# The last norm's energies summed group by group in the gelu stage, the hidden spectra fetched in four column groups, and the joined rows formed inside PSUM

## The chip, the cores and the metric

The kernel runs on one core of a Trainium2 chip. A core has TensorE (PE: matmuls; its weight loads are shown apart as PEld), VectorE (DVE), ScalarE (ACT), GpSimd (POOL) and SyncE (SP, which here only issues DMAs). The engines run their own programs and meet at semaphores. The metric is the device time of one execution in microseconds (us), lower is better.

## The reference, cut to what matters

Everything is float32. Layer 0 takes 4 x 32 images of 128 x 128 pixels and works on low-frequency Fourier spectra (33 columns x 64 rows, complex). The part that the change touches is its end:

```
a  = inorm(p + xa)                                   # p: attention result, xa: input
m  = gelu(inorm(spectral_conv(an, m0cw)) + m0sw * an)        # "hidden" image, an = inorm(a)
m  = inorm(spectral_conv(m, m1cw)) + m1sw * m                # m1: second convolution
x1 = x + inorm(m) * mon_w + mon_b + a                        # layer 0 output
```

An inorm needs the mean and the variance of every image. They are not taken from pixels: by Parseval's theorem the variance of `spectral_conv(m, m1cw)` is the sum over the spectrum of |w|^2 |Y|^2, and its covariance with m is the sum of Re(w) |Y|^2, where Y is the spectrum of the hidden image and w the weights of m1. The sums run over 33 x 64 complex coefficients of each image, with column 0 weighted once, the others twice, and column 0 symmetrised.

## The kernel before

The program is a row of stages, each a block that all engines enter and leave together through a barrier. Within a block, what each engine does is written out in order; nothing else schedules it. Three stages matter.

**Stage 5, the gelu stage** (blocks from L1432 on) walks over the 128 images in 16 groups of 8 (`GI = 8`; group g is quarter u of batch b, g = 4b + u). For each group, in the names of the code:

- POOL `stage` copies the group's spectra from `room` to `ts` (2 buffers, L1457).
- PE `inverse_h` transforms back over rows into PSUM `pz` (L1381), ACT `rows_back` copies to `zs` (L1512), PE `inverse_w` gives pixels in PSUM `pi` (L1389).
- DVE `scale` prepares `pre` from the DMA-loaded `mg` (L1556), DVE `add` adds `pi` (L1562), ACT `gelu` makes the hidden image in `yall` (L1531), and its Square into `sq` (L1534) is summed per image by DVE `sum_squares` (L1567).
- The hidden image is transformed forward: PE `forward_h` into `pf` (L1481), ACT `forward_copy` into `even`, `odd` (L1519, L1520), PE `forward_w` into `pq`, `pw` (L1488, L1489), ACT `sines_copy` (L1526), DVE `copy_out` combines both into the spectrum `yo` (66 x 8 x 64; L1575 to L1577).
- POOL `store` writes `yo` to DRAM `ys` (L1462). SP loads `mg` ahead (L1438) and fetches each batch of four groups back with an image per partition, `yt`, in one DMA per batch (L1443).

The helper `lagged(b, u, k, f)` calls f for group g - k in the turn of group g. So in its turn of group g, ACT does rows_back(g), forward_copy(g-1), gelu(g) with its Square, sines_copy(g-1). DVE does scale(g), sum_squares(g-1), add(g), copy_out(g-1). PE does inverse_h(g), forward_h(g-1), inverse_w(g), forward_w(g-1). POOL does stage(g), store(g-2). An engine takes its list strictly in this order.

**Stage 6, the last norm** (from L1620 on). DVE multiplies `yt` by the weights of m1 in four column groups (`product`, L1107 to L1111, five instructions each) into `zp`. ACT squares and sums `zp` (L1120) and scales the attention spectrum `pa` by its factor g in one pass of 128 x 4224 (L1659). DVE sums zp times yt for the covariance (L1703, L1704). Column 0 goes through PE and back to be symmetrised (L1630, L1632). Two square roots are served by ACT (L180). Then DVE joins `zp * r + pa` in five pieces (`rows_ready`, L1725), PE transposes the 33 columns (L1640), and ACT copies them to `tt`, a view of `room` (L1675). One more matmul spreads a factor (L1644).

**Stage 7** starts with the block after it (SP L1776) and reads `tt`, `yall` and the factors. **Stage 4**, ahead of stage 5, ends like the new stage 6: PE multiplies the columns of `zp` with a diagonal matrix `dg` (L1204), ACT copies the result (L1280).

Of the kernel before, what the change touches and what calls it, by code (L numbers as in the profile page):

```python
# [9 lines left out]
ALU = mybir.AluOpType  # L10
# [34 lines left out]
def constants():  # L45
# [12 lines left out]
    c["ph"] = np.concatenate([np.cos(tp), -np.sin(tp[:, 1:])], 1) / 128  # L58
    c["eh"] = np.concatenate([np.concatenate([np.cos(ph).T, -np.sin(ph).T], 0), np.concatenate([np.sin(ph).T, np.cos(ph).T], 0)], 1)
# [99 lines left out]
class Root:  # L159
# [47 lines left out]
def build(nc, a, c, out):  # L207
# [37 lines left out]
    with top:  # L245
# [1149 lines left out]
        s_yt = sem("hidden_columns_loaded")  # L1395
        s_qh, s_mg7 = sem("p7_matrix_loaded"), sems("p7_images_loaded", 2)
        with ExitStack() as p5:
# [15 lines left out]
            yo = sb("yo5", [2 * KW, GPB, GI, KH])  # L1413
# [10 lines left out]
            s_f1, s_e1, s_f2, s_e2, s_yo = sem("p5_h_transform_done"), sem("p5_h_transform_copied"), sem("p5_w_transform_done"), sem("p5_w_transform_copied"), sems("hidden_spectrum_stored", GPB)  # L1424
# [5 lines left out]
            @block.sync  # L1430
            def _(sp):
                sp.dma_start(ph[:, :], c["ph"]).then_inc(s_ph, 16)  # L1432

                def load(b):
                    for u in range(GPB):
                        g = GPB * b + u
                        wait(sp, s_m5, g + 1 - GPB)
                        sp.dma_start(mg[:, u], mixr[:, bass.ds(g * GI, GI), :]).then_inc(s_mg[u], 16)  # L1438

                def hidden_back(b):  # L1440
                    for q in s_yo:
                        sp.wait_ge(q, 16 * (b + 1))
                    sp.dma_start(yt[32 * b:32 * b + 32].rearrange("p w r h -> p (w r h)"), ys[32 * b:32 * b + 32].rearrange("i m k -> i (m k)")).then_inc(s_yt, 16)  # L1443
                load(1)
                sp.dma_start(room[:, 2 * M2:4 * M2], bass.AP(mpl.tensor, 2 * M2, [[0, 128], [1, 2 * M2]])).then_inc(s_m1, 16)
                load(2)
                hidden_back(0)
                load(3)
                for b in range(1, NB):
                    hidden_back(b)  # L1450

            @block.gpsimd
            def _(pool):
                def stage(b, u):
                    g = GPB * b + u
                    wait(pool, s_s1, g - 1)
                    nc.gpsimd.tensor_copy(ts[:, u % 2], tt[:, :, bass.ds(g * GI, GI)]).then_inc(s_ts, 1)  # L1457

                def store(b, u):
                    g = GPB * b + u  # L1460
                    pool.wait_ge(s_e2, g + 1)
                    pool.dma_start(ys[bass.ds(g * GI, GI)].rearrange("i m k -> m i k"), yo[:, u]).then_inc(s_yo[u], 16)  # L1462
# [6 lines left out]
                store(NB - 1, GPB - 2)  # L1469
                store(NB - 1, GPB - 1)  # L1470
                for q in s_yo:
                    pool.wait_ge(q, 16 * NGRP // GPB)

            @block.tensor
            def _(pe):
# [27 lines left out]
                pe.wait_ge(s_sn, NGRP)  # L1503
                nc.tensor.matmul(pq[:, 0:1], ysq[:, :], ones[:, 0:1], start=True, stop=True).then_inc(s_q5, 1)

            @block.scalar
            def _(act):
# [27 lines left out]

                def body(b):
                    for u in range(GPB):
# [6 lines left out]
                sines_copy(NB - 1, GPB - 1)  # L1544

            @block.vector
            def _(dve):
# [41 lines left out]
                ch = Chain(dve, s_v5)  # L1589
                ch.link(V.tensor_scalar(v1("ysq"), pq[:, 0:1], 1.0 / (HH * WW), None, ALU.mult))  # L1590
# [3 lines left out]
        with ExitStack() as p6:  # L1594
# [8 lines left out]
            tx = sb("t6x", [128, 2, 9, 2, KH])  # L1603
            ta = sb("t6a", [128, 2, 9 * 2 * KH])
            cs = sb("cs6", [128, 128])
            en = sb("en6", [128, 8])
            cr = sb("cr6", [128, 8])
            dg = sb("dg6", [128, NI])
            ps = [pb(f"ptr6_{i}", [128, 512]) for i in range(4)]
            psy = pb("psy6", [128, 512])  # L1610
            pbc = pb("pbc6", [128, 512])
            s_z, s_en = sem("p6_products_ready"), sem("p6_energy_sums_done")
            s_sa, s_cs, s_sc = sem("p6_column0_transposed"), sem("p6_column0_copied"), sem("p6_column0_symmetrised")
            s_pg, s_zp = sem("attention_spectrum_scaled"), sem("p6_spectrum_ready")
# [13 lines left out]
            def _(pe):  # L1628
                pe.wait_ge(s_z, 1)
                nc.tensor.transpose(psy[:, 0:128], zp[:, 0].rearrange("p r h -> p (r h)"), ident[:, :]).then_inc(s_sa, 1)  # L1630
                pe.wait_ge(s_cs, 1)
                nc.tensor.matmul(psy[:, 128:256], cs[:, :], sym[:, :], start=True, stop=True).then_inc(s_sc, 1)  # L1632
                n = 0
                for q, chunks in enumerate(ROWS):
                    pe.wait_ge(s_zp, q + 1)
                    for j in chunks:
                        lo, hi = kw_of(j)
                        wait(pe, s_trc, n - 3)
                        for kw in range(lo, hi):
                            m = nc.tensor.transpose(ps[n % 4][:, 128 * (kw - lo):128 * (kw - lo) + 128], zp[:, kw].rearrange("p r h -> p (r h)"), ident[:, :])  # L1640
                        m.then_inc(s_tr, 1)
                        n += 1
                pe.wait_ge(s_dg, 1)
                nc.tensor.matmul(pbc[:, 0:128], ones[:, :], dg[:, :], start=True, stop=True).then_inc(s_bc, 1)  # L1644

            @block.scalar
            def _(act):
                A = nc.scalar

                def squares(n, src, col, scale=1.0):  # L1650
                    size = math.prod(src.shape[1:])
                    square_sum(act, s_en, n, ta[:, n % 2, 0:size], src, en[:, col:col + 1], scale)

                def product_energy(g, n):
                    lo, hi = max(COLS[g][0], 1), COLS[g][1]
                    act.wait_ge(s_z, g + 1)
                    squares(n, zp[:, lo:hi].rearrange("p w r h -> p (w r h)"), g, ROOT2)
                A.activation(v1("warm6"), ident[:, 0:1], ACT.Sqrt)
                A.activation(pa[:, :, :, :], pa[:, :, :, :], ACT.Copy, scale=v1("g")).then_inc(s_pg, 1)  # L1659
                product_energy(0, 1)  # L1660
                act.wait_ge(s_sa, 1)
                A.activation(cs[:, :], psy[:, 0:128], ACT.Copy).then_inc(s_cs, 1)
                act.wait_ge(s_sc, 1)
                squares(2, psy[:, 128:256], 4)
                squares(3, psy[:, 128:256].rearrange("p (r h) -> p r h", r=2)[:, :, 32], 5)
                for g in range(1, len(COLS)):
                    product_energy(g, g + 3)
                root.serve(act, A, v1("r"))
                root.serve(act, A, v1("t"))
                n = 0  # L1670
                for chunks in ROWS:
                    for j in chunks:
                        lo, hi = kw_of(j)
                        act.wait_ge(s_tr, n + 1)
                        A.activation(tt[:, lo:hi], ps[n % 4][:, 0:128 * (hi - lo)].rearrange("p (j i) -> p j i", i=NI), ACT.Copy).then_inc(s_trc, 1)  # L1675
                        n += 1
                act.wait_ge(s_trc, NC6)

            @block.vector
            def _(dve):  # L1680
                ch = Chain(dve, s_v6)
                V = nc.vector
                r, t, var = v1("r"), v1("t"), v1("var")
                w1, yb_, rest, mean = scalar["m1sw"], v1("ybar"), v1("rest"), v1("offset")
                dve.wait_ge(s_m1, 16)
                for g, (lo, hi) in enumerate(COLS):
                    if g == 0:
# [545 lines left out]
```

## Time and profile before

| | us |
|---|---|
| median of 3 runs | 1052.03 (1050.84 to 1057.9) |
| the profiled execution, device time | 1055.65 |
| its span in the trace | 1054.0 |
| stage 5, first POOL instruction to the last SP issue | 417.52 to 541.45 |
| stage 6, first instruction (ACT) to the first of stage 7 | 542.96 to 580.07 |

| engine | PE | PEld | DVE | ACT | POOL |
|---|---|---|---|---|---|
| busy us of the span | 804.5 | 593.1 | 678.4 | 403.8 | 320.8 |

In a timeline row, the first number is the start in us from the span's start, the second the duration or extent, then engine, source line, operation, what it writes <- what it reads, the shapes, and how many instructions the row merges. In brackets stands how long the engine had been idle before and what ended the wait. A float32 matmul appears as two records. A transpose appears as one.

### The profile page before, as it was taken

The numbers are of one execution on the slowest core, as the hardware profiler recorded it, in microseconds if no ns is written. First come the engines' busy times: TensorE is split into PE (matmuls) and PEld (weight loads), VectorE is DVE, ScalarE is ACT, GpSimd is POOL, SyncE is SP. The second block draws the span as 40 slices with busy tenths as digits, with TensorE's granted clock in tenths as the row PEclk, the third lists the DMA queues.
The fourth block names the chain that finished last, engine by engine and source line by source line (L and its number), as shares of the span: only waits on it lengthen the run. The fifth ranks groups of instructions, "written<-read, shape, count | busy, mean of one in ns | idle before, by whom it ended". The sixth has DMA issues, their size and how long they took to land. (4 is left out here: it accounts for less than half of the span.)

```text
span 1054.0 us, 36890 instructions
## 1 busy us (share of the span) xinstructions
PE 804.5 (76%) x16113; PEld 593.1 (56%) x16113; DVE 678.4 (64%) x1459; ACT 403.8 (38%) x915; POOL 320.8 (30%) x198
## 2 busy tenths in 40 slices
PE   0499296899999955999932899566778777777797
PEld 0366142322222215888822899566777776776786
DVE  4898388778888785466648999745555555553122
ACT  0298252122222344466543566433333333331121
POOL 0023373789999900111100000232222222210000
PEclk9999598799999976899965999878998899898899
DMA  9566643376555430255330676489999999998687
GB/s 365 118 194 159 132 82 105 116 271 190 174 182 176 140 81 5 66 181 122 84 79 0 171 190 179 99 189 252 278 285 286 283 289 284 282 281 178 190 243 210
DMA packets 284673, 189.44 MB, mean 180 GB/s; under 512 B 29396, under 2 KB 275893, under 8 KB 283381
## 3 DMA queue, kind: packets, MB, share of 16 engines
q1 hardware_dynamic: 207411, 139.95, 49.3%
q10 hardware_dynamic: 75138, 44.14, 16.6%
q0 software_dynamic: 2048, 4.36, 2.0%
q8 instruction: 45, 0.74, 0.3%
q14 instruction: 31, 0.25, 0.1%
HBM read 154.50 MB, written 33.07 MB: 178 GB/s over the span
## 5 line engine op out<-in xcount | busy, mean ns | idle before, releaser
L2036 PE MATMUL po<-pa,room 128*32 128x16 f32 x8320 | 147.7, 219 | 66.4 <-DMA room<-_L_conv_weight_imag_dram 36.6
L2036 PEld LDWEIGHTS po<-pa,room 128*32 128x32 f32 x8320 | 144.9, 163 | 74.5 <-issue 63.3
L981 POOL TENSOR_TENSOR q<-lead 128x1536 f32<-128x1536 f32 (+1 forms) x51 | 170.3, 3367 | 29.4 <-POOLq L650 13.8
L1080 DVE TENSOR_TENSOR q<-pw,lead 128x1536 f32<-128x1536 f32 (+1 forms) x85 | 140.9, 1704 | 16.9 <-PE acc L1026 11.9
L1989 POOL COPY cols<-y 128x512 f32<-128x512 f32 x32 | 36.7, 1147 | 324.8 <-PE px L2023 184.8
L1026 PE MATMUL acc<-q,pt 128*32 128x384 f32 (+1 forms) x1088 | 104.2, 495 | 13.1 <-DVE q L1080 13.1
L2177 DVE TENSOR_TENSOR osl<-po,neg 128x128 f32<-128x128 f32 x64 | 18.4, 288 | 133.1 <-ACT neg L2110 133.1
L2110 ACT ACTIVATE neg<-po 128x272 f32<-128x272 f32 x32 | 12.7, 398 | 179.8 <-issue 166.6
L2023 PE MATMUL px<-wbat,cols 128*32 128x130 f32 x2176 | 78.0, 297 | 3.0 <-DVE wbat L2148 3.0
L1026 PEld LDWEIGHTS acc<-q,pt 128*32 128x32 f32 x1088 | 28.1, 110 | 87.5 <-issue 58.3
L2023 PEld LDWEIGHTS px<-wbat,cols 128*32 128x32 f32 x2176 | 68.4, 121 | 3.7 <-DVE wbat L2148 3.1
L1381 PE MATMUL pz<-eh,ts 128*33 128x128 f32 x1024 | 65.6, 282 | 6.0 <-DMA ph<-const_ph_dram 3.7
L920 ACT ACTIVATE ms<-pm,vec 128x512 f32<-128x512 f32 x32 | 22.0, 689 | 123.5 <-PE pm L913 116.1
L1389 PE MATMUL pi<-cw,zs 97*128 97x128 f32 x512 | 65.8, 283 | 2.4 <-ACT zs L1512 1.1
L1381 PEld LDWEIGHTS pz<-eh,ts 128*33 128x33 f32 x1024 | 57.1, 141 | 14.4 <-issue 8.3
L1389 PEld LDWEIGHTS pi<-cw,zs 97*128 97x128 f32 x512 | 61.3, 196 | 4.9 <-ACT zs L1512 3.0
L2202 DVE TENSOR_TENSOR yall<-yall,po 128x1024 f32 (+1 forms) x16 | 19.5, 1222 | 57.9 <-PE po L2064 57.9
L2159 DVE COPY pa<-px 32x260 f32<-32x260 f32 x128 | 49.6, 425 | 5.0 <-PE px L2023 3.6
L885 DVE TENSOR_TENSOR room<-gt,tp 128x1408 f32<-128x1408 f32 x26 | 41.3, 1619 | 8.0 <-PE psc L832 4.4
L2099 ACT ACTIVATE pa<-px 32x260 f32<-32x260 f32 x128 | 41.2, 369 | 9.0 <-PE px L2023 8.3
L392 POOL DMA_DIRECT2D xs<-xst x16 | 14.6, 910 | 93.3 <-ACT xst L426 93.3
L1462 POOL DMA_DIRECT2D ys<-yo x16 | 13.2, 824 | 97.6 <-DVE yo L1577 97.6
(334 smaller groups left out, 1540.3 us busy)
## 6 DMA issues: line engine op xcount, KB each, us to landing
room<-_L_conv_weight_real_dram ACTq DMA_DIRECT2D x32, 520.0 KB, 8.4
room<-_L_conv_weight_imag_dram ACTq DMA_DIRECT2D x32, 520.0 KB, 11.2
room<-_L_conv_weight_real_dram SPq DMA_DIRECT2D x32, 520.0 KB, 6.3
room<-_L_conv_weight_imag_dram SPq DMA_DIRECT2D x32, 520.0 KB, 9.6
lead<-xns SPq DMA_DIRECT2D x64, 192.0 KB, 3.0
lead<-wv SPq DMA_DIRECT2D x16, 576.0 KB, 5.9
yall<-in_x_dram SPq DMA_DIRECT2D x4, 2048.0 KB, 14.6
xd<-in_x_dram SPq DMA_DIRECT2D x16, 512.0 KB, 4.2
```

Of the source, the lines that this page charges most:

```text
L885: V.tensor_tensor(z[:, j % 2, :, 0:NDV], bc(bc(w, 1, NB), 3, NT), bc(xx, 2, NDV), ALU.mult).then_inc(s_z, 1)
L920: nc.scalar.activation(ms[:, u], pm[u][:, :], ACT.Identity, bias=v1("cbeta")).then_inc(s_mc, 1)
L981: nc.gpsimd.tensor_tensor(q2[:, t % 2, :, :, 0:m], bc(weights(blk, n), 2, NB), spectra(blk), ALU.mult).then_inc(s_qp, 1)
L1026: e = nc.tensor.matmul(acc[u][rows, 0:3 * m].rearrange("p (r m) -> p r m", r=3), pt[:, k, rows], qk[:, :, b, 0:m], start=(k == 0), stop=(k ...
L1080: V.tensor_tensor(q1[:, t % 2, :, :, 0:m], bc(pw[t % 4][:, 0:3 * m].rearrange("p (r m) -> p r m", r=3), 2, NB), spectra(blk), ALU.mult).th ...
L1381: m = nc.tensor.matmul(pz[64 * v:64 * v + KW, 128 * i:128 * i + 128], ts[:, u % 2, :, i], eh[:, 128 * v:128 * v + 128], start=True, stop=True)
L1389: m = nc.tensor.matmul(pi[:, 128 * i:128 * i + 128], zs[0:KP, u % 2, i, :], cw[:, :], start=True, stop=True)
L1989: nc.gpsimd.tensor_copy(cols[:, u, 0:2], near if c_ < NCHK - 1 else y1v[:, 0:64:63])
L2023: m = nc.tensor.matmul(px[u][g:g + 32, o:o + 2 * KWF], cols[:, u, q if p == 0 else 3 - q, s, 32 * b:32 * b + 32], wbat[:, b, at:at + 2 * K ...
L2036: e = nc.tensor.matmul(po[u][32 * g:32 * g + 32, 512 * q + 16 * m:512 * q + 16 * m + 16], wsl[u][:, :, q * KWF + KWF - 1 - kw], xsl[u][:, ...
L2099: act.activation(re[:, b].rearrange("i q c w -> i q (c w)"), src[:, b].rearrange("i q c w -> i q (c w)"), ACT.Copy)
L2159: V.tensor_copy(re[:, b].rearrange("i q c w -> i q (c w)"), src[:, b].rearrange("i q c w -> i q (c w)"))
```

## The change

Stage 5:

- The weights of m1 are loaded once more in the layout of `yo` (`tab`), and DVE turns them into two tables `wgt` in 12 small steps (`energy_weights`, in the turn of group 1): |w|^2 and Re(w), with column 0 symmetrised.
- For each group, ACT squares `yo` into `yq` (`square`, lag 2), POOL multiplies `yq` with both tables into `ye` and, in place, `yq` (`weigh`, lag 2), DVE sums each over the rows into `part` (`sum_energies`, two reduces, lag 3). `yo` and `yq` have two buffers, `ye` one. At the end PE sums `part` over its 66 partitions with the weights `mw` in two matmuls: variance and covariance are there when stage 5 ends.
- The store of `yo` moves from POOL to SP. SP issues load(t+4) and store(t-2) in turn t, and the fetch of `yt` as four DMAs per batch, one per column group.

Stage 6 loses all energy sums, the column-0 round trip, the scaling of `pa` and the joins on DVE. For each of the 33 columns PE now adds `pa * diag(g)` and `zp * diag(r)` in PSUM (two matmuls), plus one small matmul for the mean. The columns are taken in the order `TURN`, with six PSUM banks. The first square root needs nothing of `yt`.

```diff
             @block.gpsimd
             def _(pool):
...
-                def store(b, u):
-                    g = GPB * b + u
-                    pool.wait_ge(s_e2, g + 1)
-                    pool.dma_start(ys[bass.ds(g * GI, GI)].rearrange("i m k -> m i k"), yo[:, u]).then_inc(s_yo[u], 16)
+                def weigh(b, u):
+                    g = GPB * b + u
+                    pool.wait_ge(s_yq, g + 1)
+                    if g == 0:
+                        pool.wait_ge(s_wt5, 1)
+                    wait(pool, s_ws, g)
+                    v = yq[:, u % 2]
+                    nc.gpsimd.tensor_tensor(ye[:, :, :], v, bc(wgt[:, 0], 1, GI), ALU.mult)
+                    nc.gpsimd.tensor_tensor(v, v, bc(wgt[:, 1], 1, GI), ALU.mult).then_inc(s_we, 1)
 
                 def body(b):
                     for u in range(GPB):
                         lagged(b, u, 0, stage)
-                        lagged(b, u, 2, store)
+                        lagged(b, u, 2, weigh)
...
             @block.scalar
+                def square(b, u):
+                    g = GPB * b + u
+                    act.wait_ge(s_e2, g + 1)
+                    wait(act, s_ws, g - 1)
+                    act.activation(yq[:, u % 2], yo[:, u % 2], ACT.Square).then_inc(s_yq, 1)
...
                         lagged(b, u, 1, sines_copy)
+                        lagged(b, u, 2, square)
...
             @block.vector
+                def sum_energies(b, u):
+                    g = GPB * b + u
+                    dve.wait_ge(s_we, g + 1)
+                    V.reduce_sum(part[:, 0, bass.ds(g * GI, GI)], ye[:, :, :], axis=AX.X)
+                    V.reduce_sum(part[:, 1, bass.ds(g * GI, GI)], yq[:, u % 2], axis=AX.X).then_inc(s_ws, 1)
...
                         lagged(b, u, 1, copy_out)
+                        if b == 0 and u == 1:
+                            energy_weights()
+                        lagged(b, u, 3, sum_energies)
                 each_batch(body)
                 sum_squares(NB - 1, GPB - 1)
                 copy_out(NB - 1, GPB - 1)
+                for n in (3, 2, 1):
+                    sum_energies(NB - 1, GPB - n)
...
             @block.tensor
-                            m = nc.tensor.transpose(ps[n % 4][:, 128 * (kw - lo):128 * (kw - lo) + 128], zp[:, kw].rearrange("p r h -> p (r h)"), ident[:, :])
+                def rows(n):
+                    pe.wait_ge(s_z, PART_OF[TURN[n]] + 1)
+                    wait(pe, s_trc, n - NBANK + 1)
+                    for kw, o in slots(n):
+                        nc.tensor.matmul(o, pa[:, kw].rearrange("p r h -> p (r h)"), dg[:, 0, :], start=True, stop=False)
+                        m = nc.tensor.matmul(o, zp[:, kw].rearrange("p r h -> p (r h)"), dg[:, 1, :], start=False, stop=(kw > 0))
...
```

The order of instructions shows three places. POOL, stage 5, after the first two copies of `ts`; `ys` and `ye` are the stored spectra and the weighted squares. Before:

```order
L1457 COPY ts<-room 128x264 [waits p5_rows_done]
L1462 DMA ys<-yo 66x8x64 [waits p5_w_transform_copied]
L1457 COPY ts<-room 128x264 [waits p5_rows_done]
L1462 DMA ys<-yo 66x8x64 [waits p5_w_transform_copied]
L1457 COPY ts<-room 128x264 [waits p5_rows_done]
```

The same place of the change:

```order
L1483 COPY ts<-room 128x264 [waits p5_rows_done]
L1492 TENSOR_TENSOR ye<-yq,wgt 66x512 [waits hidden_energies_summed,hidden_spectrum_squared]
L1493 TENSOR_TENSOR yq<-yq,wgt 66x512
L1483 COPY ts<-room 128x264 [waits p5_rows_done]
L1492 TENSOR_TENSOR ye<-yq,wgt 66x512 [waits hidden_energies_summed,hidden_spectrum_squared]
```

Between two copies of `ts`, the issue of a store has given way to two products, and they wait for ACT's square and for DVE's sums.

ACT, stage 5, from the third gelu on in the change (before, the row L1573 is not there, and the others stand in the same order):

```order
L1564 ACTIVATE yall<-pre 128x1024 [waits p5_preactivation_ready]
L1567 ACTIVATE sq<-yall 128x1024 [waits hidden_squares_summed,hidden_ready]
L1559 ACTIVATE sines<-pq 66x256 [waits p5_w_transform_sines_done]
L1573 ACTIVATE yq<-yo 66x512 [waits p5_w_transform_copied]
L1545 ACTIVATE zs<-pz 97x1024 [waits p5_pixels_done,p5_rows_done]
L1552 ACTIVATE even<-pf 128x264 [waits p5_w_transform_done,p5_h_transform_done]
```

The square of `yo` stands behind the gelu, its Square and the sines of the same turn, and ahead of the next `rows_back`.

DVE, stage 5, one turn of the change, from `add` to the next `add` (before, the two reduces of `ye` and `yq` are not there):

```order
L1604 TENSOR_TENSOR pre<-pre,pi 128x1024 [waits p5_mixed_scaled,p5_pixels_done]
L1619 COPY yo<-pw 66x8 [waits hidden_spectrum_squared,p5_sine_part_copied,hidden_spectrum_stored_0,p5_w_transform_done]
L1620 TENSOR_TENSOR yo<-pw,sines 66x8x31
L1621 TENSOR_TENSOR yo<-pw,sines 66x8x32
L1646 TENSOR_REDUCE part<-ye 66x8 [waits hidden_energies_weighted]
L1647 TENSOR_REDUCE part<-yq 66x8
L1598 TENSOR_TENSOR pre<-mg,c1b 128x1024 [waits hidden_ready,p5_mixed_loaded_0]
L1609 TENSOR_REDUCE ysq<-sq 128x8 [waits hidden_squared]
L1604 TENSOR_TENSOR pre<-pre,pi 128x1024 [waits p5_mixed_scaled,p5_pixels_done]
```

The sums stand behind `copy_out` and ahead of the next `scale`.

## Rows read from the trace of the kernel before

**Rows 1.** Waits, 445 to 535 us: engine line <- releaser: us, times, longest us.
```profile
POOL ys L1462 <- DVE yo L1577: 77.9, 14, 6.0
```
**Rows 2.** Timeline, one period of stage 5, part of its rows.
```profile
446.81 0.41 POOL L1457 COPY ts<-room 128x264 f32<-128x264 f32 x1
447.87 1.20 DVE L1562 TENSOR_TENSOR pre<-pre,pi 128x1024 f32<-128x1024 f32 x1
448.59 1.97 PE L1381 MATMUL pz<-eh,ts 128*33 128x128 f32 x32
449.10 1.06 ACT L1531 ACTIVATE yall<-pre 128x1024 f32<-128x1024 f32 x1 [2.66 <-DVE pre L1562]
450.19 1.06 ACT L1534 ACTIVATE sq<-yall 128x1024 f32<-128x1024 f32 x1
...
451.16 0.36 ACT L1526 ACTIVATE sines<-pq 66x256 f32<-66x256 f32 x1
451.42 1.01 ACT L1512 ACTIVATE zs<-pz 97x1024 f32<-97x1024 f32 x1
451.62 0.17 DVE L1575 COPY yo<-pw 66x8 f32<-66x8 f32 x1 [2.55 <-ACT sines L1526]
...
452.36 1.21 DVE L1556 TENSOR_TENSOR pre<-mg,c1b 128x1024 f32<-128x1024 f32 x1
452.48 2.05 PE L1389 MATMUL pi<-cw,zs 97*128 97x128 f32 x16
...
453.49 1.21 DVE L1567 TENSOR_REDUCE ysq<-sq 128x8 f32<-128x1024 f32 x1
...
454.62 1.21 DVE L1562 TENSOR_TENSOR pre<-pre,pi 128x1024 f32<-128x1024 f32 x1
```
**Rows 3.** Timeline, stage 5: POOL's copy for group 3, ACT's gelu of group 2.
```profile
440.10 0.41 POOL L1457 COPY ts<-room 128x264 f32<-128x264 f32 x1
...
442.35 1.06 ACT L1531 ACTIVATE yall<-pre 128x1024 f32<-128x1024 f32 x1 [2.63 <-DVE pre L1562]
```
**Rows 4.** Groups by line and shape, POOL: count | busy us, mean ns | idle before.
```profile
L981 POOL TENSOR_TENSOR q<-lead 128x1536 f32<-128x1536 f32 x48 | 164.9, 3464 | 27.7 <-POOLq L650 13.8 <-PE acc L1026 10.5 <-DMA lead<-wv 3.4
...
L763 POOL TENSOR_TENSOR room<-gt,xrm 128x640 f32<-128x640 f32 x26 | 33.0, 1270 | 12.8 <-PE psc L832 12.8
```
**Rows 5.** Timeline, start of stage 5, PE.
```profile
426.84 3.64 PE L1381 MATMUL pz<-eh,ts 128*33 128x128 f32 x32
```
**Rows 6.** Windows: us, busy (count) of PE, PEld, DVE, ACT, POOL; PEclk; DMA share, GB/s.
```profile
404.50:410.00 5.50, 5.32 (x25) 5.32 (x26) 4.91 (x11) 1.19 (x2) 0.00 (x0) 0.50 0.00 0
410.00:415.00 5.00, 5.00 (x46) 5.00 (x46) 0.00 (x0) 3.15 (x6) 0.00 (x0) 0.99 0.00 0
...
537.00:545.00 8.00, 0.00 (x0) 0.00 (x0) 0.61 (x3) 2.03 (x3) 0.81 (x1) 0.50 0.44 96
```
**Rows 7.** Timeline, end of stage 5 and stage 6, part of its rows.
```profile
537.13 0.41 DVE L1577 TENSOR_TENSOR yo<-pw,sines 66x256 f32<-66x256 f32 x1
...
541.15 0.30 SPq L1443 DMA_DIRECT2D yt<-ys  x1
...
542.96 1.28 ACT L1658 ACT_TABLE_LOAD   x1 [6.73 <-PEq L1397]
...
546.06 0.69 DVE L1107 TENSOR_TENSOR t<-room,yt 128x512 f32<-128x512 f32 x1 [8.45 <-DMA yt<-ys]
...
550.23 0.16 DVE L1694 TENSOR_TENSOR vec<-vec 128x1 f32<-128x1 f32 x1
...
552.74 0.69 DVE L1107 TENSOR_TENSOR t<-room,yt 128x512 f32<-128x512 f32 x1
...
556.53 1.06 ACT L1120 ACTIVATE t6a<-zp 128x1024 f32<-128x1024 f32 x1 [3.94 <-DVE zp L1111]
...
573.99 0.60 ACT L1675 ACTIVATE room<-ptr 128x512 f32<-128x512 f32 x1 [3.11 <-PE ptr L1640]
...
580.07 0.36 SPq L1776 DMA_DIRECT2D pa<-mixd  x1
```

More of the change, by code:

```diff
@@ L1432, in _, with load @@
                 sp.dma_start(ph[:, :], c["ph"]).then_inc(s_ph, 16)
-                def load(b):
-                    for u in range(GPB):
-                        g = GPB * b + u
-                        wait(sp, s_m5, g + 1 - GPB)
-                        sp.dma_start(mg[:, u], mixr[:, bass.ds(g * GI, GI), :]).then_inc(s_mg[u], 16)
+                def load(g):
+                    wait(sp, s_m5, g + 1 - GPB)
+                    sp.dma_start(mg[:, g % GPB], mixr[:, bass.ds(g * GI, GI), :]).then_inc(s_mg[g % GPB], 16)
@@ L1445, in _ @@
[L1445 to L1450, printed above, removed]
+                        sp.wait_ge(q, 16 * (GPB // 2) * (b + 1))
+                    for (lo, hi), q in zip(COLS, s_yt):
+                        sp.dma_start(yt[32 * b:32 * b + 32, lo:hi].rearrange("p w r h -> p (w r h)"),
+                                     ys[32 * b:32 * b + 32, 2 * lo:2 * hi].rearrange("i m k -> i (m k)")).then_inc(q, 16)
@@ new lines, in _ @@
+                for r in range(2):
+                    sp.dma_start(tab[:, r], bass.AP(mpl.tensor, 2 * M2 + r * M2, [[KH, KW], [0, 2], [1, KH]])).then_inc(s_tb, 16)
+                sp.dma_start(mw[:, :], c["mw"]).then_inc(s_tb, 16)
+                for t in range(NGRP + 2):
+                    if t + GPB < NGRP:
+                        load(t + GPB)
+                    if t == 1:
+                        sp.dma_start(room[:, 2 * M2:4 * M2], bass.AP(mpl.tensor, 2 * M2, [[0, 128], [1, 2 * M2]])).then_inc(s_m1, 16)
+                    if t >= 2:
+                        store(t - 2)
+                        if (t - 1) % GPB == 0:
+                            hidden_back((t - 1) // GPB - 1)
@@ L1466, in body @@
                         lagged(b, u, 0, stage)
-                        lagged(b, u, 2, store)
+                        lagged(b, u, 2, weigh)
                 each_batch(body)
[L1469 to L1472, printed above, removed]
+                weigh(NB - 1, GPB - 2)
+                weigh(NB - 1, GPB - 1)
             @block.tensor
@@ L1503, in _ @@
                 pe.wait_ge(s_sn, NGRP)
+                pe.wait_ge(s_ws, NGRP)
+                pe.wait_ge(s_tb, 48)
+                for i in range(2):
+                    nc.tensor.matmul(pq[:, i + 1:i + 2], part[:, i, :], mw[:, :], start=True, stop=True)
                 nc.tensor.matmul(pq[:, 0:1], ysq[:, :], ones[:, 0:1], start=True, stop=True).then_inc(s_q5, 1)
@@ L1648, in _ @@
                 A = nc.scalar
[L1650 to L1657, printed above, removed]
-                A.activation(v1("warm6"), ident[:, 0:1], ACT.Sqrt)
[L1659 to L1667, printed above, removed]
+                A.activation(v1("warm6"), ident[:, 0:1], ACT.Sqrt)
                 root.serve(act, A, v1("r"))
                 root.serve(act, A, v1("t"))
[L1670 to L1677, printed above, removed]
+                for n, j in enumerate(TURN):
+                    lo, hi = kw_of(j)
+                    act.wait_ge(s_tr, n + 1)
+                    A.activation(tt[:, lo:hi], ps[n % NBANK][:, 0:128 * (hi - lo)].rearrange("p (j i) -> p j i", i=NI), ACT.Copy).then_inc(s_trc, 1)
+                act.wait_ge(s_trc, len(TURN))
             @block.vector
```

174 lines of the change are left out of this document (97 added, 77 removed).

## The prediction

> **What bounds the kernel now.** The kernel is a row of stages with barriers between them, so the time is the sum of the stages, and a stage is worth what its own longest wait is worth. I read the engines' shares first, then the waits of stage 5, then its timeline over one period, and last the timeline of stage 6.
>
> Stage 5 repeats every 6.75 us: DVE's `add` starts at 447.87 and again at 454.62 [rows 2]. Two things share that period. One is a loop over ACT and DVE: add to gelu 1.23, gelu to sines 2.06, sines to `copy_out` 0.46, `copy_out` to `scale` 0.74, `scale` to `sum_squares` 1.13, and 1.13 more to the next add. That is 6.75, without slack. The other is PE, which starts `inverse_w` at 452.48, on the heels of the matmuls ahead of it. The reader should look above all at who runs beside whom. PE starts `inverse_h` of group G+1 at 448.59, *before* ACT starts the gelu of group G at 449.10, because POOL had copied the spectra of G+1 at 446.81. POOL looks as if it had room: it waited 77.9 us in this stretch for `yo` [rows 1].
>
> Stage 6 takes 37.1 us from 542.96 to 580.07, of which DVE waits until 546.06 for `yt` (idle 8.45 in all). The rest is nearly all DVE [rows 7].
>
> **The change part by part.** The sum is made against the profiled execution (span 1054.0, device time 1055.65). The median of the runs is 3.6 lower, and I carry the difference over to it.
>
> *The loop that closes.* POOL's list is now stage(G+1) behind weigh(G-2). weigh(G-2) waits for ACT's square(G-2), which stands in ACT's list behind gelu(G), its Square and the sines, and it waits for DVE's sum_energies(G-3), which stands behind add(G) and copy_out(G-1). Both need pixels of group G, which need inverse_h(G), which needs stage(G). So stage(G+1) cannot start before nearly all of group G has passed through every engine. The store that stood there before needed only copy_out(G-2), one turn earlier. Queued behind the waiting POOL instruction is the copy of `ts`, and PE waits for that. Nothing else runs meanwhile but DVE's `scale` and `sum_squares`. The period becomes the length of this chain:
>
> - copy of `ts` 0.41 and 0.1 to hand over; inverse_h to inverse_w 3.89 (448.59 to 452.48, with forward_h of the group before between them); inverse_w to add 2.14; add to gelu 1.23; gelu to sines 2.06; sines to copy_out 0.46; copy_out to the next DVE instruction 0.74 [rows 2]. Together 11.0.
> - Two reduces of 66 x 512. A reduce of 1024 elements a partition takes 1.21 and lets the next start after 1.13 [rows 2]. A 512-element multiply takes 0.69 [rows 7]. Bounds: 0.57 and 0.69 each, I take 0.6, with 0.1 to hand over: 1.3.
> - Two POOL products of 66 x 512. The trace has products of 640 elements at 1.27 and of 1536 at 3.46 [rows 4], that is 1.02 and 1.15 each for 512. I take 1.1: 2.2.
>
> Sum: 14.5 us with TensorE at its full clock.
>
> *The clock.* PE now idles some 7 us in each period. In 537 to 545, with PE idle, the granted clock is 0.50. A burst that begins at 404.68 in such a state runs at 0.50 until 410, about 5.4 us, and at 0.99 after that [rows 6]. At half clock inverse_h takes 3.64 for 1.97 [rows 5, 2], a factor 1.85. So I let each burst do its first 5.4 us at half speed, which is 2.9 us of work, and lose 2.5: the period is 17.0. The bounds are no fall at all (14.5) and half clock for all 5.94 us of inverse_h, forward_h and inverse_w (plus 5.0: 19.6).
>
> *How long stage 5 gets.* The 12 small table steps delay turn 2 by about 2.6 (at 0.16 and a hand-over each, the row at 550.23 [rows 7]), so the gelu of group 2 goes from 442.35 [rows 3] to about 445.0. Sines at 447.0, square from 447.3 to 447.9 (a 512-element ACT copy takes 0.60 [rows 7]), weigh(0) to 450.2. Then the copy for group 3 starts, which before started at 440.10 [rows 3]. From it to the end of weigh(13) there are 13 periods, 221.0 us, to 671.2. The tail is serial, since `ye` has one buffer: three sums and two products, 3 x 1.3 + 2 x 2.3 = 8.5. The last matmuls and three one-column copies, 1.8 by the same small rows, and the barrier, 1.5 (541.45 to 542.96 [rows 7]). Stage 6 starts at 683.0 and not 542.96: **+140.0**.
>
> *Edits at nothing.* The two extra table loads and SP's stores lie on SP, whose turn is far shorter than the period. ACT's square and the square roots lie inside the chain as counted. `yt` lands during the serial tail, so stage 6 no longer waits for it. If it came late, the old wait of at most 3.1 (542.96 to 546.06) would be back.
>
> *Stage 6.* DVE: about 3.2 of small steps and the wait for the ACT table load (1.28), 1.4 of small steps, the first product 3.9 (552.74 to 556.53 is 3.8 [rows 7]), 1.0 for the factors. PE starts near 9.6. The products end at 10.4 + 3.8 + 3.8 + 4.6 = 22.6. PE now does 132 records for 33 columns where there were 33 transposes. A record of this shape costs 0.213 at half clock (25 in 5.32) and 0.109 at full (46 in 5.00) [rows 6], so four columns cost 3.4 or 1.7. The first two steps at half clock end at 17.6 (the second waits for its product), half of the third is slow too, and the other steps run at full clock: PE ends near 30.0, the stage at 30.7. Bounds: 26 at full clock, 38 at half. Gain 37.1 - 30.7: **-6.4**. With DVE done at 22.6, PE sets the end of the stage.
>
> Sum: 1055.65 + 140.0 - 6.4 = 1189.3 for the profiled kind, and 1052.03 + 133.6 = **1186** for the median.
>
> *A rule weighed.* No row shows POOL working beside a DVE instruction with both operands in SBUF. weigh(G-2) would: DVE's `scale` of the next group (mg and c1b, both in SBUF, 1.13 to the next start [rows 2]) starts when the sums end. The Trainium skill, "GPSIMD Engine Reference", section 8 (Key points), says that POOL shares its SBUF interfaces with VectorE and contends with DVE instructions that have two SBUF inputs. By the rule weigh would grow by up to the 1.13 of `scale`, and the sum would be 1201; without it, 1186. The same list says that VectorE is about twice as fast at elementwise work, which speaks against putting the products on POOL at all.
>
> **The rivals.**
>
> 1. *Forecast*: the loop closes through POOL, half clock for part of each burst. 1186. Chance 0.48.
> 2. *Full clock throughout*: 13 x 2.5 less, 1153. For it: before 404.68 PE had idled far longer than 7 us. Against: 8 idle us were enough for 0.50 in 537 to 545. 0.12.
> 3. *Half clock throughout*: 13 x 2.6 more, 1220. For it: the bursts have about 6 us of chained work, little more than the 5.4. 0.18.
> 4. *POOL slowed beside DVE*: `scale` and weigh share a resource, 13 x 1.13 more, 1201. 0.10.
> 5. *No closed loop*: POOL keeps its lead, and only DVE's own loop grows by the two reduces to 8.0. Then 16 x 1.2 + 2.6 + some 6 of tail - 6.4: 1074. It needs POOL's copy not to be held behind the products, against the rows of the order. 0.07.
> 6. *The other side*: the sums go into DVE's idle 2.55 before `copy_out` [rows 2] and the period stays 6.75. Then only stage 6 counts: 1052 - 6.4 = 1046, or 1041 at full clock. It is decided by the period: above 7.1 (6.4/16 more) it is lost. The sums stand behind `copy_out` and not ahead of it. 0.03.
>
> **How the numbers follow.** The range takes in cases 1 to 4 (0.88): 1150 to 1222. About 1% is what a measurement here can tell from no change. Slower by over 1%: cases 1 to 5 and what is left of unforeseen, 0.95. Within 1%: 0.03. Faster: 0.02.
>
> **What would show it right or wrong.** In the profile after: the copy of `ts` should start after the two products, and those after the second reduce; `inverse_h` of G+1 after `copy_out` of the turn of G. The period of `add` in stage 5 should be 17.0 (14.5 to 19.6), with PE busy under half of it and the granted clock between 0.5 and 1. The two products should take 1.02 to 1.15 us each; over 1.5 speaks for rival 4. Stage 6 should last about 31, with no wait for `yt`. If the period is near 8, the reading of POOL's list is wrong, and with it all of the forecast; if stage 6 is much shorter than 26, the clock was higher than assumed.

## The result, and the profile after

| | before | after |
|---|---|---|
| median of 4 runs, us | 1051.43 (1049.73 to 1057.9) | 1189.26 (1186.2 to 1189.85, and one of 1232.89) |
| ratio | | 1.1287, 95% interval 1.1254 to 1.132 |
| span of the profiled execution | 1054.0 | 1188.1 |
| stage 5, first POOL instruction to stage 6 | 417.52 to 542.96: 125.4 | 419.09 to 685.06: 266.0 |
| stage 6 | 37.1 | 685.06 to 712.76: 27.7 |
| all behind stage 6 | 473.9 | 475.3 |

(The run of 1232.89 had a granted clock of 0.83 where the other three had 0.86 to 0.87, and is left out of the ratio.) Of the spans: stage 5 lost 140.5, stage 6 won 9.4, and the rest moved by 3, since stage 5 started 1.6 later and what stands behind stage 6 is 1.4 longer.

First the waits of the changed kernel from 460 to 660 us, most of stage 5, columns as in [rows 1].

```profile
POOL ye L1492 <- DVE part L1647: 160.0, 12, 13.4
PEld pz L1390 <- POOL ts L1483: 111.6, 12, 9.3
...
ACT zs L1545 <- PE pz L1390: 100.0, 11, 9.1
```

In [rows 1] POOL waited for `yo`, and in that view of the kernel before no engine waits for POOL. Now PE's weight loads wait 9.3 us per period for POOL's copy, ACT and DVE wait for PE, and POOL waits 13.4 for DVE's sums. That is a ring of waits: each engine waits for the next, and the last of them for the first. Its timeline, one period late in the stage, to be held against [rows 2]:

```profile
639.81 0.39 POOL L1483 COPY ts<-room 128x264 f32<-128x264 f32 x1
640.25 3.19 PEld L1390 LDWEIGHTS pz<-eh,ts 128*33 128x33 f32 x32 [9.30 <-POOL ts L1483]
640.25 3.59 PE L1390 MATMUL pz<-eh,ts 128*33 128x128 f32 x32 [8.83 <-POOL ts L1483]
643.77 1.86 PEld L1510 LDWEIGHTS pf<-ph,yall 128*128 128x128 f32 x16 [0.33 <-issue]
...
645.61 2.00 PE L1398 MATMUL pi<-cw,zs 97*128 97x128 f32 x16
...
647.65 1.22 DVE L1604 TENSOR_TENSOR pre<-pre,pi 128x1024 f32<-128x1024 f32 x1 [9.01 <-PE pi L1398]
...
648.90 1.06 ACT L1564 ACTIVATE yall<-pre 128x1024 f32<-128x1024 f32 x1 [2.43 <-DVE pre L1604]
...
650.96 0.36 ACT L1559 ACTIVATE sines<-pq 66x256 f32<-66x256 f32 x1
651.22 0.62 ACT L1573 ACTIVATE yq<-yo 66x512 f32<-66x512 f32 x1
651.45 0.17 DVE L1619 COPY yo<-pw 66x8 f32<-66x8 f32 x1 [2.58 <-ACT sines L1559]
...
652.18 0.67 DVE L1646 TENSOR_REDUCE part<-ye 66x8 f32<-66x512 f32 x1
652.77 0.67 DVE L1647 TENSOR_REDUCE part<-yq 66x8 f32<-66x512 f32 x1
653.37 1.21 DVE L1598 TENSOR_TENSOR pre<-mg,c1b 128x1024 f32<-128x1024 f32 x1
653.59 2.11 POOL L1492 TENSOR_TENSOR ye<-yq,wgt 66x512 f32<-66x512 f32 x1 [13.39 <-DVE part L1647]
...
655.67 1.25 POOL L1493 TENSOR_TENSOR yq<-yq,wgt 66x512 f32<-66x512 f32 x1
656.87 0.40 POOL L1483 COPY ts<-room 128x264 f32<-128x264 f32 x1
657.32 3.59 PE L1390 MATMUL pz<-eh,ts 128*33 128x128 f32 x32 [8.83 <-POOL ts L1483]
```

Apart from `scale` (653.37) and the square (651.22, done well before the products), these rows follow one another. From copy to copy it is 17.06 us, where before it was 6.74. The rows from 640.25 to 648.90 are inverse_h, inverse_w, `add` and gelu of one and the same group. inverse_h of the next group starts at 657.32, 8.4 us *behind* that gelu, where before it started 0.5 ahead of it. The clock in the same period, windows as in [rows 6]:

```profile
640.50:643.50 3.00, 3.00 (x32) 2.62 (x28) 0.00 (x0) 0.00 (x0) 0.00 (x0) 0.50 0.00 0
644.00:648.50 4.50, 4.49 (x36) 3.86 (x35) 0.85 (x1) 1.58 (x3) 0.00 (x0) 1.00 0.00 0
651.00:657.00 6.00, 0.00 (x0) 0.00 (x0) 4.26 (x7) 0.83 (x3) 3.41 (x3) 0.50 0.10 23
```

inverse_h runs at half clock, the matmuls behind it at full clock. Stage 6, part of its timeline, against [rows 7]:

```profile
685.07 1.28 ACT L1728 ACT_TABLE_LOAD   x1 [9.89 <-PEq L1406]
...
689.28 0.68 DVE L1116 TENSOR_TENSOR t<-room,yt 128x512 f32<-128x512 f32 x1
...
694.04 0.77 PE L1711 MATMUL ptr<-dg,pa 128*128 128x128 f32 x2 [10.05 <-DVE dg L1771]
...
697.83 0.60 ACT L1734 ACTIVATE room<-ptr 128x512 f32<-128x512 f32 x1 [8.23 <-PE ptr L1712]
...
705.97 0.48 DVE L1120 TENSOR_TENSOR zp<-zp,t 128x320 f32<-128x320 f32 x1
...
712.76 0.36 SPq L1818 DMA_DIRECT2D pa<-mixd  x1
```

The first product starts 4.2 us into the stage without a wait for `yt`. DVE is done with the products at 706.45, and PE's chain of pairs ends the stage. PE's clock in it:

```profile
694.00:698.00 4.00, 3.75 (x16) 3.49 (x16) 3.90 (x9) 0.17 (x1) 0.00 (x0) 0.50 0.00 0
698.00:702.00 4.00, 3.69 (x33) 3.69 (x34) 3.97 (x7) 1.03 (x2) 0.00 (x0) 0.97 0.00 0
```

### The profile page after: what moved, and what is told of

The parts are those of the page before. It is cut to its first block and busy times, and to the rows that moved or that the text cites. A ratio compares the mean times of both kernels' runs of the same rounds, so it can differ in the third digit from the quotient of the medians.

```text
span 1188.1 us, 37212 instructions
## 1 busy us (share of the span) xinstructions
PE 833.6 (70%) x16215; PEld 616.9 (52%) x16215; DVE 691.6 (58%) x1495; ACT 404.4 (34%) x917; POOL 356.7 (30%) x214
## 5 line engine op out<-in xcount | busy, mean ns | idle before, releaser
L990 POOL TENSOR_TENSOR q<-lead 128x1536 f32<-128x1536 f32 (+1 forms) x51 | 170.3, 3364 | 30.1 <-POOLq L659 13.8
L1390 PE MATMUL pz<-eh,ts 128*33 128x128 f32 x1024 | 86.7, 340 | 121.6 <-POOL ts L1483 115.8
L1390 PEld LDWEIGHTS pz<-eh,ts 128*33 128x33 f32 x1024 | 71.2, 155 | 136.1 <-POOL ts L1483 121.9
L1604 DVE TENSOR_TENSOR pre<-pre,pi 128x1024 f32<-128x1024 f32 x16 | 19.5, 1221 | 125.0 <-PE pi L1398 125.0
L1492 POOL TENSOR_TENSOR ye<-yq,wgt 66x512 f32<-66x512 f32 x16 | 30.4, 1898 | 201.7 <-DVE part L1647 176.3
L1545 ACT ACTIVATE zs<-pz 97x1024 f32<-97x1024 f32 x16 | 16.4, 1022 | 121.3 <-PE pz L1390 121.3
L2244 DVE TENSOR_TENSOR yall<-yall,po 128x1024 f32 (+1 forms) x16 | 19.5, 1221 | 57.8 <-PE po L2106 57.8
```

Source lines behind the costliest of these rows:

```text
L990: nc.gpsimd.tensor_tensor(q2[:, t % 2, :, :, 0:m], bc(weights(blk, n), 2, NB), spectra(blk), ALU.mult).then_inc(s_qp, 1)
L1390: m = nc.tensor.matmul(pz[64 * v:64 * v + KW, 128 * i:128 * i + 128], ts[:, u % 2, :, i], eh[:, 128 * v:128 * v + 128], start=True, stop=True)
L1492: nc.gpsimd.tensor_tensor(ye[:, :, :], v, bc(wgt[:, 0], 1, GI), ALU.mult)
L2244: V.tensor_tensor(y, y, po[u % 2][:, :].rearrange("h (b o w) -> h b o w", b=NB, o=2), ALU.add).then_inc(s_fin, 1)
```

## The experiments

All edits are to the changed kernel. The period is the distance between two `add`s of DVE late in stage 5, where it is steady; by the same measure the kernel before has 6.78 (6.75 at the place of [rows 2]). The kernel before, run beside these, had a median of 1053.5, and ratios are taken to it.

| run | edit | period | time | forecast time |
|---|---|---|---|---|
| changed kernel | | 17.06 | 1189.3 | |
| e1 | POOL's copy one group ahead | 7.97 | 1074.3 | 1071 |
| e2 | sums behind scale | 17.07 | 1187.7 | 1193 |
| e3 | 30 filler matmuls | 17.07 | 1190.1 | 1169 |
| e4 | sums and square earlier, POOL as it was | 13.65 | 1140.9 | 1135 |
| e5 | e1 and e4 together | 7.17 | 1060.1 | 1050 |
| e6 | and the tables early | 7.17 | 1057.4 | 1046 to 1048 |
| e7 | 36 filler matmuls | 15.47 | 1168.9 | 1170 |
| e8 | e2 and e7 | 15.75 | 1175.1 | e7 + 4 |
| e9 | e6, scale behind sum_squares | 6.98 | 1054.6 | 1052 |
| e10 | e9 with two buffers for ye | 6.98 | 1052.0 | 1050.5 |

Of e2, e3, e4, e7 and e8 there is one run each; what is said of them rests on the rows of the period, not on the time.

**e1: is it the order of POOL's list?**

```diff
                     for u in range(GPB):
-                        lagged(b, u, 0, stage)
+                        if GPB * b + u + 1 < NGRP:
+                            stage(b + (u + 1) // GPB, (u + 1) % GPB)
                         lagged(b, u, 2, weigh)
+                stage(0, 0)
                 each_batch(body)
```

> The changed kernel with one edit: in POOL's list the copy of ts for group g+1 stands ahead of the products of group g-2, not behind them. Theory 1 (a closed loop through POOL's list sets the period): the copy no longer waits for the gelu of the group before, TensorE runs beside the gelu again, and the period falls from 17.05 us to DVE's own loop, 6.75 + 1.2 = 8.0; 13 periods save 9.05 each, so 1189 - 118 = 1071. Theory 2 (the added work itself, squares, products and sums, is what costs): the work is all still there, so the time stays above 1150. TensorE should be at its full clock in the stage by theory 1.

Measured 1074.28, ratio to the kernel before 1.0194 (1.0155 to 1.0233), period 7.97. All the added work is still there, and 115 of the 138 us are gone: the kernel is about 2% slower than before. Timeline of e1:

```profile
492.70 1.21 DVE L1606 TENSOR_TENSOR pre<-pre,pi 128x1024 f32<-128x1024 f32 x1
...
493.94 1.06 ACT L1566 ACTIVATE yall<-pre 128x1024 f32<-128x1024 f32 x1 [2.90 <-DVE pre L1606]
493.96 0.40 POOL L1483 COPY ts<-room 128x264 f32<-128x264 f32 x1
...
494.42 1.97 PE L1390 MATMUL pz<-eh,ts 128*33 128x128 f32 x32 [1.35 <-POOL ts L1483]
...
497.82 0.67 DVE L1649 TENSOR_REDUCE part<-yq 66x8 f32<-66x512 f32 x1
...
500.67 1.21 DVE L1606 TENSOR_TENSOR pre<-pre,pi 128x1024 f32<-128x1024 f32 x1
```

inverse_h (494.42) runs beside the gelu (493.94) again, in 1.97 us; the granted clock is 1.00 from 470 to 540. What is left of the period, 7.97 - 6.78 = 1.19, is what the two reduces take in DVE's own loop. Theory 2 falls.

**e4: does the ring shrink by what is taken out of it?**

```diff
                         lagged(b, u, 0, add)
+                        lagged(b, u, 3, sum_energies)
                         lagged(b, u, 1, copy_out)
...
-                        lagged(b, u, 3, sum_energies)
...
                         lagged(b, u, 1, forward_copy)
+                        lagged(b, u, 2, square)
                         lagged(b, u, 0, gelu)
                         lagged(b, u, 1, sines_copy)
-                        lagged(b, u, 2, square)
```

> The changed kernel with two moves that leave POOL's list as it is: DVE's sums of group g-3 stand between add and copy_out (where DVE waits 2.55 us anyway), and ACT's square of group g-2 stands ahead of the gelu. The loop through POOL is still closed, since the products still wait for sums that stand behind add, but it is shorter: gelu, its Square, sines and copy_out (1.25 + 2.06 + 0.49 + 0.73 less an add's 1.13 to the next instruction, 3.4) leave it, and so does the slow product beside scale (0.85). Theory 1: period about 12.9, time about 1189 - 13 x 4.2 = 1135. Theory 2 (the added work itself costs): no less work, so no change, 1189.

Period 13.65 and not 12.9, time 1140.9: the mechanism as forecast, 0.75 short. Timeline of e4:

```profile
586.71 1.22 DVE L1604 TENSOR_TENSOR pre<-pre,pi 128x1024 f32<-128x1024 f32 x1 [6.40 <-PE pi L1398]
...
588.45 0.67 DVE L1647 TENSOR_REDUCE part<-yq 66x8 f32<-66x512 f32 x1
589.26 1.26 POOL L1492 TENSOR_TENSOR ye<-yq,wgt 66x512 f32<-66x512 f32 x1 [9.82 <-DVE part L1647]
...
591.25 1.59 DVE L1598 TENSOR_TENSOR pre<-mg,c1b 128x1024 f32<-128x1024 f32 x1
591.70 1.40 POOL L1483 COPY ts<-room 128x264 f32<-128x264 f32 x1
...
600.37 1.22 DVE L1604 TENSOR_TENSOR pre<-pre,pi 128x1024 f32<-128x1024 f32 x1 [6.40 <-PE pi L1398]
```

The products take 1.26 each, but now the copy meets `scale`: 1.40 for 0.40, and `scale` 1.59 for 1.21. The 1.0 of the copy more than covers the 0.75; inverse_h gives 0.2 back, with 3.41 for 3.59 (its clock falls in every period here too, see e8).

**e2: who slows the product?**

```diff
                         lagged(b, u, 0, scale)
+                        lagged(b, u, 4, sum_energies)
                         lagged(b, u, 1, sum_squares)
...
-                        lagged(b, u, 3, sum_energies)
```

> The changed kernel with DVE's two sums moved behind scale of the next group, so that POOL's products run beside sum_squares (one operand in SBUF) and no longer beside scale (two). In the changed kernel one product took 2.11 us beside scale, the other 1.25. If it is the instruction beside it that slows POOL: both products take 1.26, the chain loses 0.85 and gains scale's 1.13, the period goes from 17.05 to 17.3, and the time rises by 4 us to about 1193. If the first product is slow for its own sake (its operands): it stays at 2.11, the period is 18.2, and the time about 1204.

Beside a reduce the same product took 1.26, in every period. Timeline of e2:

```profile
600.47 1.21 DVE L1609 TENSOR_REDUCE ysq<-sq 128x8 f32<-128x1024 f32 x1
600.70 1.26 POOL L1492 TENSOR_TENSOR ye<-yq,wgt 66x512 f32<-66x512 f32 x1 [14.25 <-DVE part L1647]
```

So the neighbour was the cause, 2.11 beside `scale` (two operands in SBUF), 1.26 beside `sum_squares` (one). But the period did not rise to 17.3. It was 17.07, within 0.01 of the changed kernel's. e8 takes this up.

**e3 and e7: what does the clock cost?** Both add matmuls to PE's idle time, into `pf`, whose content is overwritten before it is read (30 in e3, 36 in e7):

```diff
                         lagged(b, u, 1, forward_w)
+                        if GPB * b + u > 1:
+                            for _ in range(30):
+                                nc.tensor.matmul(pf[:, 0:128], ident[:, :], eh[:, 0:128], start=True, stop=True)
```

> The changed kernel with 30 matmuls of 128 x 128 by 128 columns added to every turn from the third on, behind forward_w, into the PSUM tile pf, whose content is not read before forward_h overwrites it. They take 30 x 0.224 = 6.7 us of TensorE's 8.8 idle us and nobody waits for them. If the half clock costs what the changed kernel's rows show (inverse_h 3.45 us where it takes 1.9 at full clock): the granted clock in the stage goes from 0.72 to about 1, the period from 17.05 to 15.5, and the time to 1189 - 13 x 1.5 = 1169. If the slow inverse_h came from elsewhere (POOL or DVE beside it), nothing changes, 1189.

A miss: period 17.07 again. Windows of e3, columns as in [rows 6]:

```profile
599.50:601.50 2.00, 0.00 (x0) 0.00 (x0) 0.52 (x1) 0.00 (x0) 2.00 (x3) 1.00 0.00 0
602.00:605.00 3.00, 3.00 (x32) 2.44 (x28) 0.00 (x0) 0.00 (x0) 0.00 (x0) 0.50 0.02 5
605.50:616.50 11.00, 11.00 (x95) 10.59 (x94) 4.90 (x8) 4.36 (x7) 1.53 (x1) 1.00 0.06 13
```

With 2.1 us of idle time left ahead of inverse_h, the clock still stood at full through it, fell just after inverse_h had begun, and was back for what came behind. The expectation of e3 was wrong in taking 2 idle us for harmless. Its period and time are those of its other case (inverse_h slowed by a neighbour, 1189), but the windows show the clock fallen, and no DVE, ACT or POOL busy beside inverse_h. e7 tests it.

> The changed kernel with 36 filler matmuls a turn where e3 had 30. In e3 TensorE was idle only 2.1 us ahead of inverse_h, and still the granted clock fell to half 0.3 us after inverse_h had begun and came back 3.4 us later, as in the changed kernel; the period was 17.07 in both. With 36 (8.1 us) less than 1 us of idle time is left. If that keeps the clock up: inverse_h 1.97 us, period 17.07 - 1.5 = 15.6, time 1189 - 19 = 1170. If inverse_h is slow for another reason than the clock: 1189 again.

```profile
594.41 8.20 PE L1528 MATMUL pf<-eh,ident 128*128 128x128 f32 x72
603.42 1.97 PE L1390 MATMUL pz<-eh,ts 128*33 128x128 f32 x32 [0.81 <-POOL ts L1483]
```

That is PE's timeline in e7. With 0.81 us idle, the granted clock is 1.00 from 470 to 640, inverse_h takes 1.97, the period is 15.47 and the time 1168.9. The half clock costs 1.6 us a period, some 20 us over 13 periods. That the time fell by 20 as well is in part chance: the fillers lengthen the tail of stage 5 by 4.8 (from the last gelu to stage 6: 23.9 for 19.1), and in this one run stage 5 also started 2.8 earlier.

**e8: why did e2's edit cost nothing?**

> e2 and e7 together: sums behind scale, and 36 filler matmuls. In e2 the chain lost 0.85 us at POOL and gained 1.13 at DVE, yet its period was 17.06 as in the changed kernel, with the clock falling at another place of the period. If the half clock takes up such differences (a later start of inverse_h means a shorter stretch of it at half clock), then at full clock the edit shows its own price: period 0.3 above that of e7, 15.9, and about 4 us more in all. If the two edits simply cost nothing, the period equals that of e7.

Period 15.75 against e7's 15.47: +0.28, as worked out for e2 (1.13 - 0.85). At full clock the edit shows its price. With a clock that falls and comes back in every period, it did not: e2's inverse_h took 3.30 us in place of 3.59, as a shorter part of it lay ahead of the return of the clock. The periods themselves show that they settle on a value. From the fourth on they are 16.88, 16.98, 17.02, 17.04 and 17.06 us in the changed kernel, which comes from below; 17.18, 17.13, 17.09 and 17.08 in e2, which comes from above; and 13.75, 13.70 and 13.67 down to 13.65 in e4; e3 has 17.06 at once. e7 and e8, whose clock stays up, have 15.47 and 15.76 at once. So e4's 13.65 may be such a settled value too, and its terms (1.0 and 0.2 above) need not be the price of its edits at full clock. What sets these values is not shown.

**e5, e6, e9, e10: how much of the work can be hidden?**

> Three moves together: POOL's copy of ts one group ahead (as in e1), DVE's sums between add and copy_out, ACT's square ahead of the gelu (as in e4). In e1 the period was 7.97 us, DVE's loop of 6.75 with the sums' 1.2 in it. Here the sums lie in the 2.55 us that DVE waits for the sines anyway, and the square in ACT's 2.66 idle us ahead of the gelu. Theory 1: the period is that of the kernel before, 6.75 to 6.8; the stage keeps only the tables' 2.5 us and a tail about 5 us longer than before, stage 6 saves 9.4 (37.1 to 27.7), so the time is about 1050, the same as before. If the added work costs through shared resources (POOL's products beside DVE, ACT at its limit), the period stays above 7.3 and the time above 1058.

Measured 1060.05, ratio 1.0069 (1.0044 to 1.0093): 10 us above the forecast, a miss. The period was 7.17, not 6.8, which makes some 5.5 of the 10. The tail, from the last gelu to stage 6, takes 19.5 us for 12.5 before, where 5 more were expected: another 2.

e6 moves `energy_weights()` behind the first `scale` and the sums of group 13 ahead of the last `copy_out`:

> As e5, with DVE's 12 table steps moved into turn 0, where DVE waits 7 us for the first pixels, and in the tail the sums of group 13 ahead of the last copy_out. Theory 1: the 2.5 us of the tables leave the path, and about 1 of the tail: 3.5 below e5, about 1046 to 1048, some 0.5% below the kernel before. If the table loads land too late (after 427 us), nothing is gained over e5.

1057.43, ratio 1.0036 (1.0015 to 1.0057). 2.6 below e5 for the 3.5 forecast, with the same period. Timeline of e6:

```profile
506.09 1.59 DVE L1600 TENSOR_TENSOR pre<-mg,c1b 128x1024 f32<-128x1024 f32 x1
...
506.55 1.40 POOL L1483 COPY ts<-room 128x264 f32<-128x264 f32 x1
...
508.74 1.21 DVE L1606 TENSOR_TENSOR pre<-pre,pi 128x1024 f32<-128x1024 f32 x1
```

The copy meets `scale` again, and here `scale` is in DVE's loop: 1.59 for 1.21 is 0.38, and the period is 7.17 - 6.78 = 0.39 too long. e9 swaps `scale` and `sum_squares`:

```diff
+                        lagged(b, u, 1, sum_squares)
                         lagged(b, u, 0, scale)
                         if b == 0 and u == 0:
                             energy_weights()
-                        lagged(b, u, 1, sum_squares)
```

> As e6, with DVE's scale and sum_squares of a turn swapped. In e5 and e6 the period was 7.17 us: POOL's copy of ts (1.40 us where it takes 0.40 alone) ran beside scale, and scale took 1.60 where it takes 1.21. With the swap the copy should lie beside the reduce (one operand in SBUF). If the pair of copy and scale is what the period of 7.17 was made of: scale 1.21, copy 0.4, period 6.78, 14 x 0.39 = 5.5 us less than e6, about 1052, not to be told from the kernel before (1053.5). If the period was made of something else (TensorE, ACT with its square), it stays 7.17 and the time 1057.

Timeline of e9, then its waits from 450 to 530:

```profile
506.10 1.21 DVE L1611 TENSOR_REDUCE ysq<-sq 128x8 f32<-128x1024 f32 x1
506.56 0.40 POOL L1483 COPY ts<-room 128x264 f32<-128x264 f32 x1
507.22 1.21 DVE L1600 TENSOR_TENSOR pre<-mg,c1b 128x1024 f32<-128x1024 f32 x1
```

```profile
PEld pi L1398 <- ACT zs L1547: 4.3, 12, 0.4
```

Both durations are back, the period is 6.98, the time 1054.6 and the ratio 1.0005 (0.9987 to 1.0023). The last 0.2 a period goes with a wait of PE's weight loads for ACT's `rows_back`, 4.3 us in 12 turns; the same wait in the kernel before came to 1.4 in 9 turns, 0.2 at most. That this wait is the cause was not tested.

> As e9, with two buffers for the weighted squares ye (the second shares its memory with the table loads, which are used up by then). In the tail POOL's products of group 15 then need not wait for the sums of group 14: about 1.3 us less, 1050.5. In the loop nothing should change, unless the products, which now may start as soon as ACT's square is there, come to lie beside scale: then they take 2.1 for 1.26, which POOL can afford, and scale 1.2 to 1.6, which DVE can not; the period would go back to 7.1 and the time to 1056.

1051.96, ratio 0.9994 (0.9975 to 1.0013). The product did come to lie beside `scale`, and took 2.28, but `scale` itself stayed at 1.21 and the period at 6.98, where the expectation had both rise. The difference to e9 lies within the intervals. So the best order found makes the change as fast as the kernel before, not faster.

Where the gain of stage 6 went can be read from the profiled execution of e10 (span 1055.5 for 1054.0). From the start of stage 5 to the last gelu it takes 3.1 us more (14 periods of 0.2), the tail 2.6 more (15.2 for 12.5; 16.5 in e9), and what stands behind stage 6 2.6 more. And stage 6 itself took 30.1 us, not the 27.7 of the changed kernel, so it won 7.0 and not 9.4. The clock in it:

```profile
558.00:562.00 4.00, 3.61 (x16) 3.31 (x16) 3.93 (x9) 0.35 (x1) 0.00 (x0) 0.50 0.00 0
562.00:566.00 4.00, 3.87 (x18) 3.87 (x19) 3.97 (x8) 0.30 (x2) 0.00 (x0) 0.50 0.00 0
```

Its pairs of matmuls start at 557.86, and the clock is still at half 8 us later. In the changed kernel, whose stage 6 has the same instructions, it was back 4 us after 694.04. Stage 6 takes 27.7 us in the profiles of the changed kernel, e1, e2, e3, e5, e7 and e8, and 29.7 to 30.1 in those of e4, e6, e9 and e10.

## Why the prediction was right

The forecast was 1186, the time is 1189.3, and the reason is the one forecast: e1 undoes the order of POOL's list alone and takes back 115 us, with the added work in place. But the sum came out better than its terms, and that part is luck.

- **The chain.** Forecast 14.5 without the clock, measured 15.47 in e7. Its terms from the copy of `ts` to the first reduce add up to 10.8 there for the 11.0 forecast; the one that was most off is inverse_h to inverse_w, 3.74 for 3.89. The reduces, 0.67 each, took 1.19 to the end of their place, and 1.41 to the first product, for 1.3.
- **POOL's products were mis-sized.** Forecast 2.2, measured 3.28 (653.59 to 656.87). Without `scale` beside it one takes 1.26, above the upper bound of 1.15 that was scaled down from the larger shapes of [rows 4]. Why this shape costs more for its size was not tested. Beside `scale` it takes 0.85 more.
- **The rule weighed** was that of the Trainium skill, "GPSIMD Engine Reference", section 8 (Key points): contention with VectorE instructions that have two SBUF inputs. The trace agrees: 2.11 beside `scale`, 1.26 beside a reduce (e2). It was given a chance of 0.10 as a rival, and happened at three quarters of its price. The runs add a case where VectorE pays too: `scale` took 1.59 beside POOL's copy of `ts` (e4, e5, e6). Beside a product it stayed at 1.21 in all turns of the changed kernel but one (1.78 at 449.95, where the product had started 0.6 ahead of it).
- **The clock was mis-sized the other way.** Forecast +2.5 from 5.4 us of half clock in each burst, measured +1.6: the clock was back by 643.8, 3.5 us after inverse_h had begun. The 5.4 came from a single burst of the kernel before; in stage 6 the same clock took 4 us to come back in one profile and over 8 in another. The errors of the products (+1.1), the reduces (+0.1), the other terms (-0.2) and the clock (-0.9) cancel, and left the period at 17.06 for 17.0.
- **Rival 2** (full clock throughout) rested on PE having idled "far longer than 7 us" ahead of 404.68. The trace of the kernel before has 7.91 us of idle time there, much the same as the 8.83 of each period after. So that row spoke against the rival and not for it.
- **Stage 5 as a whole** was +140.5 for +140.0. Its tail was 9.2 from the end of weigh(13) (673.15) to the last reduce for 8.5.
- **Stage 6** saved 9.4 for 6.4. Its half clock ended after 4 us of matmuls, not after two steps and a half. PE waited for DVE's products once more, 0.5 us ahead of the second step at 698.31, and then no more: that PE would set the end of the stage was right. DVE's work was 21.4 for 22.6. In the four profiles with the longer half clock the stage took 29.7 to 30.1, close to the 30.7 forecast. That `yt` lands in the tail, unseen, was right.
- **Rival 5** (no closed loop, 1074) is, to the microsecond, what e1 measured, with POOL's copy no longer behind the products: DVE's own loop grew to 7.97 for 8.0. **Rival 6** was wrong also on its own terms: with the sums in DVE's wait the period was 7.17 and then 6.98, not 6.75, since it had not seen the copy beside `scale`, and stage 6 took 30 us in the profiles of e6, e9 and e10.

## What to carry to other kernels

- When work is added to an engine that "has room", look at what stands behind it in that engine's list and who waits for that. A copy of 0.4 us behind two products that needed late data cost 115 us. The share of busy time (POOL 30% before and after) did not show it.
- With work at lag k on one engine, the thing behind it inherits that lag: write down for each instruction which group's results it must have seen, and compare with the group it feeds. Here the copy for group G+1 had come to depend on the gelu of group G.
- In a ring of waits a microsecond counts on whichever engine it falls. The ring made the period 10.3 us longer; with the ring opened the same work cost 1.2 of them (e1), and moved into existing waits 0.2 (e9).

## What the runs showed of the hardware that was not expected

- Where the clock falls and comes back in each period, the period settles on a value: 17.06, 17.07 and 17.07 us in three kernels whose chains differ by up to 0.3 us (changed, e2) or in PE's idle time by 6.7 us (changed, e3), and 13.65 in e4. At full clock the same edit showed its 0.28. The cause is open.
- The clock fell in each period of e3, whose PE was idle for 2.1 us ahead of inverse_h, and stood at full in e7, idle for 0.8 us there. These are two cases, not a limit.
- How long a burst stays at half clock is not a fixed time: 3.5 us in the changed kernel's inverse_h, 5.4 in the kernel before at 404.68, and 4 or over 8 for the same instructions of stage 6 (changed kernel, e10). Stage 6 took 27.7 or about 30 us by it.
- POOL and DVE slow each other by kind of neighbour: a product 1.26 alone or beside a reduce, 2.11 to 2.28 in the steady turns beside a DVE multiply of two SBUF tiles; the copy of `ts` 0.40 alone, 1.40 beside it, and then the multiply itself 1.59 for 1.21.
